# Window attention and convolution block: score rows four partitions apart, and half of the value copy on DVE

## Chip, core and metric

One NeuronCore of one Trainium2 chip runs the whole kernel in one launch. The metric is the device time of that launch in microseconds (us). Engines are named as in the profile: PE is the matrix engine (PEld its weight loads), DVE the vector engine, ACT the scalar engine, POOL the GpSimd engine, SP the queue that issues most transfers.

## What is computed

```
x: 32 x 96 x 56 x 56 float32; windows of 7 x 7 = 49 tokens; 12 heads of 8 channels
xn   = layernorm(x over channels) * g + b                  # per token
q,k,v= xn @ qkv_w.T + qkv_b
attn = softmax(q * 8**-0.5 @ k.T + bias_table[rel])        # 49 x 49 per head and window
x2   = x + (attn @ v) @ proj_w.T + proj_b
c    = batchnorm(depthwise_conv3x3(x2))
out  = c + gelu(c @ w1.T + b1) @ w2.T + b2                 # 96 -> 384 -> 96
```

## The kernel before

**Chunks and steps.** The image rows are cut into 256 chunks (CHUNKS), 8 per image; a chunk is 7 image rows, 96 channels by 392 pixels, which is 8 windows. The program is a software pipeline written out by hand, one function `step` per engine: in one step the layernorm works on chunk e, the q, k, v products on chunks e-1 and e-2, the row maxima on e-2, the exponentials and the product with v on e-3 and e-4, the projection on e-5, the convolution taps on e-6 and e-7, the two dense layers on e-7 and e-8. There are 264 steps. Eight are written out ahead, then a loop (`run`, line 168) goes 30 times over a body of eight steps and jumps back, then the rest is written out. Nothing schedules: each engine takes its instructions in the order written, and semaphores hold it.

**How the scores are made.** float32 products are split into float16 parts, high and low (`kh`, `kl`, `qh`, `ql`, each 96 rows by 512, row = d * 12 + head for the 8 elements d of a head). For one head, a score is a single matmul whose contraction rows are held in two buffers, `k_all` and `q_all`, four slots deep, [123, 4, 12 heads, 512]. The first 49 rows (and 49 rows from 64) hold the one-hot keys against the bias (high and low part); eight rows each from partition 48+, 56+ and 112+ hold the three terms high*high, low*high and high*low; two rows hold what the 48+ rows overwrite; row 122 holds the row maximum against -1. `max_scores` (line 318) uses rows 0 to 121 and gives the scores whose maxima DVE takes (`maxima`, line 671, L676); `exp_scores` (line 304) uses all rows and gives score minus maximum for ACT's exp (L501).

**The score transfers.** [...] SP issues six of them per step (`term`, line 239, issue at L242), 96 KB each, 8 destination partitions of 12 KB:

```
TERM = (48, 56, 112)
sp.dma_start(t[TERM[n]:TERM[n] + HD, c % 4, :, :], part[:, c % 2, :]).then_inc(exp_in[c % 4], 16)
```

SP's order in a step (line 244) is: the maxima row (L252), the load of x (L256), kh twice, qh twice, kl, then a wait for `y_done`, ql, and the store of y (L272). The first `max_scores` of a step waits for all six transfers of its chunk (`exp_in`). `y` (DVE, L729) is the last result of chunk e-8 and is waited for by SP before ql goes out.

**The value copy.** `values` (PE, line 387) makes v for two windows at a time, the one on PSUM partitions 0 to 48, the other on 64 to 112. ACT copies both to `v32` (L555, two ACTIVATEs), every fourth float of the destination. Then ACT squares the centred input (L560, waited for by PE's `variance`, L361), and PE's `projection` (L409) may overwrite the PSUM bank once the copy is done.

**Setup.** DVE clears `k_all`, sets rows of -1 (L624, L625), and after the loads copies the one-hot and bias rows into four slots, the two row groups apart (L661, L663, 16 copies); POOL clears `q_all`. Four small transfers then move the two spare rows (L224), and SP waits for them.

Of the kernel before, what the change touches and what calls it, by code (L numbers as in the profile page):

```python
# [7 lines left out]
F32, F16 = mybir.dt.float32, mybir.dt.float16  # L8
# [3 lines left out]
HD = C // HEADS  # L12
# [10 lines left out]
WP = 64  # L23
TERM = (48, 56, 112)
LAST = (120, 121)
MAXROW = 122
ROWS = 123
NG = HEADS // 4
# [5 lines left out]
UP = 256.0  # L34
LOADS = 22
UN = CPI


def block_program(nc, x, w_qkv, b_qkv_row, b_v, w_proj, w_proj_rows, b_proj, ln_g, ln_b, bias_q,
                  conv_w, bn_g, bn_b, bn_mean, bn_var, w1, b1, w2, b2, eye, out):  # L40
    ctx = ExitStack()
    with ctx:
# [6 lines left out]
        def sems(name, n):  # L49
# [9 lines left out]
        center, avg = sb("center", [C, C]), sb("avg", [C, C])  # L59
        hot_f, hot_h = sb("hot_f", [64 + TOK, WP]), sb("hot_h", [64 + TOK, WP], F16)  # L60
        g_c, b_c, bv_c, bng_c, bnb_c, bnm_c, bnv_c, b2_c = (cols[:, i:i + 1] for i in range(8))
# [22 lines left out]

        bias_f = p32[0:64 + TOK, 0, :, :]
        bias_h = o_sb[0:64 + TOK, 0, :, :].rearrange("p g t -> p (g t)").bitcast(F16)[:, 0:HEADS * TOK].rearrange("p (h t) -> p h t", t=TOK)
        bias_l = o_sb[64:64 + TOK, 1, :, :].rearrange("p g t -> p (g t)").bitcast(F16)[:, 0:HEADS * TOK].rearrange("p (h t) -> p h t", t=TOK)
        rows_f, wq_f = y[:, 0, 0:3 * C], y[:, 1, 0:3 * C]
# [19 lines left out]
        dve_setup, act_setup, pe_setup, pool_setup = sem("dve_setup"), sem("act_setup"), sem("pe_setup"), sem("pool_setup")  # L108
        ready, shift_done, rows_set = sem("ready"), sem("shift_done"), sem("rows_set")
        x_in = sems("x_in", 4)  # L110
# [89 lines left out]
        def _(sp):  # L200
# [79 lines left out]
        def _(pe):  # L280
# [117 lines left out]
            def projection(st):  # L398
# [85 lines left out]
        def _(act):  # L484
# [55 lines left out]
            def step(st):  # L540
# [72 lines left out]
        def _(dve):  # L613
# [39 lines left out]

            for rows in (slice(0, TOK), slice(64, 64 + TOK)):
                v.tensor_copy(hot_h[rows, :], hot_f[rows, :])
                link(v.tensor_copy(bias_h[rows, :, :], bias_f[rows, :, :]))
            link(v.tensor_tensor(bias_l, bias_f[64:64 + TOK, :, :], bias_h[64:64 + TOK, :, :], ALU.subtract))
            dve.wait_ge(pool_setup, 2)
            for r in range(4):
                for rows, part in ((slice(0, TOK), bias_h[0:TOK, :, :]), (slice(64, 64 + TOK), bias_l)):  # L660
                    v.tensor_copy(k_all[rows, r, :, :].rearrange("p h (w t) -> p (h w) t", t=WP),  # L661
                                  hot_h[rows, :].unsqueeze(1).broadcast_to([TOK, HEADS * NW, WP]))
                    v.tensor_copy(q_all[rows, r, :, :].rearrange("p h (w t) -> p h w t", t=WP)[:, :, :, 0:TOK],  # L663
                                  part.unsqueeze(2).broadcast_to([TOK, HEADS, NW, TOK]))
            for r in range(2):
# [46 lines left out]
            def step(st):  # L712
# [84 lines left out]
```

## Time and profile before

| | |
|---|---|
| three runs | 4474.67, 4489.48, 4498.07 us (median 4489.48) |
| profiled execution, own time | 4491.72 us |
| its span | 4489.9 us (1.8 us around it) |
| granted PE clock, mean | 0.941 |
| PE busy | 3754.7 us, 84% |
| ACT busy | 3323.4 us, 74% |
| DVE busy | 2753.7 us, 61% |
| POOL busy | 1201.4 us, 27% |
| queue of SP's transfers | 36.1% of 16 engines' span |

A busy share is an average over the span. `A <- B` after an idle time names what the profile takes to have ended it; "issue" means that it shows no such thing. The granted clock is 1.00 at 2.4 GHz and 0.50 at 1.2 GHz. L numbers are lines of the kernel before.

### The profile page before, as it was taken

The numbers are of one execution on the slowest core, as the hardware profiler recorded it, in microseconds if no ns is written. First come the engines' busy times: TensorE is split into PE (matmuls) and PEld (weight loads), VectorE is DVE, ScalarE is ACT, GpSimd is POOL, SyncE is SP. The second block draws the span as 40 slices with busy tenths as digits, with TensorE's granted clock in tenths as the row PEclk, the third lists the DMA queues.
The fourth block names the chain that finished last, engine by engine and source line by source line (L and its number), as shares of the span: only waits on it lengthen the run. The fifth ranks groups of instructions, "written<-read, shape, count | busy, mean of one in ns | idle before, by whom it ended". The sixth has DMA issues, their size and how long they took to land.

```text
span 4489.9 us, 198689 instructions
## 1 busy us (share of the span) xinstructions
PE 3754.7 (84%) x83724; PEld 2432.7 (54%) x83724; DVE 2753.7 (61%) x4908; ACT 3323.4 (74%) x5379; POOL 1201.4 (27%) x1550
## 2 busy tenths in 40 slices
PE   2788888888888888888888888888888888888887
PEld 1555555555555555555555555555555555555554
DVE  6466566666555666666565665666665665556666
ACT  1578777777777777777777777777777777778787
POOL 1222222222222222222222222222222222222222
PEclk9899899999889999999999988999999998899999
DMA  1444444444444444444444444444444444444442
GB/s 29 64 73 78 72 73 75 76 74 75 67 69 76 75 72 73 74 76 74 72 76 70 78 69 70 75 75 76 73 73 72 78 75 71 70 74 79 75 78 50
DMA packets 269485, 322.72 MB, mean 72 GB/s; under 512 B 54991, under 2 KB 252048, under 8 KB 268594
## 3 DMA queue, kind: packets, MB, share of 16 engines
q1 hardware_dynamic: 235826, 232.32, 36.1%
q0 software_dynamic: 32768, 77.14, 7.0%
q8 instruction: 729, 11.94, 1.3%
q14 instruction: 162, 1.33, 0.1%
HBM read 39.35 MB, written 38.54 MB: 17 GB/s over the span
## 4 chain that ended last, share of the span: by engine, by line
DMA 28%; PE 28%; issue 15%; ACT 12%; DVE 10%; SPq 6%; ACTq 0%; DVEq 0%; POOL 0%; POOLq 0%
DMA q_all<-ql 28%; SPq L242 6%; PE sm_ps L327 6%; PE a_ps L440 6%; DVE mx L676 4%; PE o_ps L343 3%; DVE s L698 3%; PE st_ps L312 2%; PE a_ps L361 2%; ACT g L538 2%; PE b_ps L285 2%; ACT sq L564 1%; ACT v L555 1%; ACT sq L566 1%; ACT sq L560 1%
## 5 line engine op out<-in xcount | busy, mean ns | idle before, releaser
L676 DVE TENSOR_REDUCE mx<-sm_ps 128x12 f16<-128x588 f32 x1024 | 782.7, 764 | 967.1 <-PE sm_ps L327 966.8
L698 DVE SCALAR_TENSOR_TENSOR s<-ximg,cols,s 96x392 f32<-96x392 f32 x2048 | 1262.0, 616 | 13.1 <-POOL s L600 2.9
L600 POOL TENSOR_TENSOR s<-ximg,cols 96x392 f32<-96x392 f32 x256 | 281.0, 1098 | 2897.9 <-DVE y L729 2897.9
L327 PEld LDWEIGHTS sm_ps<-k_all,q_all 122*64 122x64 f16 x24576 | 505.9, 118 | 605.0 <-DMA q_all<-ql 351.1
L327 PE MATMUL sm_ps<-k_all,q_all 122*64 122x49 f16 x24576 | 617.5, 197 | 254.6 <-DMA q_all<-ql 241.9
L501 ACT ACTIVATE p<-st_ps 128x588 f32<-128x588 f32 x1024 | 666.2, 651 | 208.1 <-PE st_ps L312 205.4
L440 PE MATMUL a_ps<-g,w_s 128*96 128x392 f32 x1536 | 677.7, 555 | 0.0
L607 POOL DMA_DIRECT2D ox<-o_sb x1024 | 580.7, 569 | 59.3 <-issue 39.2
L312 PE MATMUL st_ps<-q_all,k_all 123*64 123x49 f16 x24576 | 580.5, 193 | 6.3 <-issue 6.3
L312 PEld LDWEIGHTS st_ps<-q_all,k_all 123*64 123x64 f16 x24576 | 493.8, 115 | 158.8 <-issue 155.4
L343 PE MATMUL o_ps<-p,v 128*32 128x49 f32 x24576 | 439.1, 213 | 150.9 <-DVE mx L676 145.8
L735 DVE TENSOR_TENSOR xn<-d_ps,sq 96x392 f32<-96x392 f32 x256 | 143.9, 562 | 668.3 <-ACT sq L566 668.3
L343 PEld LDWEIGHTS o_ps<-p,v 128*32 128x32 f32 x24576 | 332.0, 112 | 372.5 <-DVE mx L676 181.1
L521 ACT ACTIVATE o_sb<-o_ps 128x294 f32<-128x294 f32 x512 | 213.0, 416 | 327.8 <-PE o_ps L343 327.3
L555 ACT ACTIVATE v<-b_ps 49x384 f32<-49x384 f32 x512 | 445.0, 869 | 8.8 <-PE b_ps L287 2.5
L595 POOL TENSOR_TENSOR xl<-xn,xh 96x392 f16<-96x392 f32 x256 | 332.5, 1299 | 316.0 <-ACT xh L570 315.8
L361 PE MATMUL a_ps<-sq,avg 96*96 96x392 f32 x512 | 232.7, 537 | 140.4 <-ACT sq L560 140.4
L440 PEld LDWEIGHTS a_ps<-g,w_s 128*96 128x96 f32 x1536 | 261.5, 184 | 139.2 <-issue 115.9
L544 ACT ACT_TABLE_LOAD x256 | 328.4, 1283 | 4.6
L538 ACT ACT_TABLE_LOAD x256 | 328.4, 1283 | 4.4
L432 PE MATMUL b_ps<-s,w_s 96*128 96x392 f32 x512 | 229.6, 532 | 99.0 <-issue 98.6
L570 ACT ACTIVATE xh<-xn 96x392 f16<-96x392 f32 x256 | 138.2, 540 | 160.9 <-DVE xn L735 160.9
(96 smaller groups left out, 5396.8 us busy)
## 6 DMA issues: line engine op xcount, KB each, us to landing
ox<-o_sb POOLq DMA_DIRECT2D x1024, 73.5 KB, 5.3
k_all<-kh SPq DMA_DIRECT2D x512, 96.0 KB
q_all<-qh SPq DMA_DIRECT2D x512, 96.0 KB
x_sb<-in_x SPq DMA_DIRECT2D x256, 147.0 KB, 3.5
out<-y SPq DMA_DIRECT2D x256, 147.0 KB, 7.5
k_all<-kl SPq DMA_DIRECT2D x256, 96.0 KB
q_all<-ql SPq DMA_DIRECT2D x256, 96.0 KB
q_all<-mxt SPq DMA_DIRECT2D x256, 12.0 KB, 4.1
```

The source lines that it names most:

```text
L312: last = mm(st_ps[64 * w:64 * w + 64, h // HH, c0:c0 + TOK], k_all[:, r, h, n:n + WP], q_all[:, r, h, n:n + TOK], start=True, stop=True)
L327: last = mm(sm_ps[64 * w:64 * w + 64, h // HH, c0:c0 + TOK], q_all[0:MAXROW, r, h, n:n + WP], k_all[0:MAXROW, r, h, n:n + TOK], start=True ...
L343: last = mm(o_ps[32 * c4:32 * c4 + 32, at:at + TOK], v32[:, r, h, q, :], p32[:, q, h, :], start=True, stop=True)
L440: last = mm(a_ps[0:C, 0:CT], w2_s[:, k, :], g[:, k, :], start=k == 0, stop=k == NB - 1)
L501: af(p32[:, q, :, :].rearrange("p (b h) n -> p b h n", b=2), st_ps[:, :, 0:HALF].rearrange("p b (h n) -> p b h n", n=TOK), ACT.Exp).then_i ...
L538: af(g[:, k, :], (a_ps, d_ps, b_ps)[k][:, 0:CT], ACT.Gelu, bias=b1_c[:, k:k + 1]).then_inc(g_done, 1)
L544: act.preload_act_table_set("natural_log_exp_and_others")
L555: af(v32[64 * w:64 * w + TOK, (st[1] - 2) % 2, :, :, :].rearrange("p h n (d x) -> p (h n d) x", x=4)[:, :, w], b_ps[64 * w:64 * w + TOK, 0 ...
L595: tt(xl[0:C, r, :, 0:TOK], xn[:, :, :], xh[0:C, r, :, 0:TOK], ALU.subtract).then_inc(xl_done, 1)
L607: nc.gpsimd.dma_start(ox[:, r4, x4, :], o_sb[x4::4, r4, :, :]).then_inc(o_in[r4], 16)
L676: v.tensor_reduce(mx[:, (st[1] - lag) % 2, :, p].rearrange("p (b h) -> p b h", b=2), sm_ps[:, :, 0:HALF].rearrange("p b (h n) -> p b h n", ...
L698: v.scalar_tensor_tensor(acc, image_rows(st, lag, k // 3, k % 3), cw_c[:, k:k + 1], acc, ALU.mult, ALU.add)\
```

## The change

The contraction rows are laid out anew. The three terms interleave over partitions 0 to 31: term n takes partitions n, n+4, ..., n+28 (n = 0, 1, 2). The bias rows take the rest, the high part on 64 to 112, the low part in five pieces (32 to 63, 113 to 126, and 3, 7, 11); row 127 holds the maximum. The contraction is 127 and 128 rows instead of 122 and 123. SP's order and the six sizes stay. The copy of v on partitions 64 to 112 goes from ACT to DVE, behind y and ahead of tap 8, with a semaphore of its own. In the setup, the bias and one-hot rows are laid down once over 128 partitions (8 copies instead of 16), `k_all` isn't cleared, the four row transfers and their wait are gone, there are 31 loads instead of 22, and SP waits for three small memsets before the first load.

```diff
-TERM = (48, 56, 112)
-LAST = (120, 121)
-MAXROW = 122
-ROWS = 123
+ROWS = 128
+MAXROW = ROWS - 1
+TERMS = 4 * HD
+HIGH = ((2 * TERMS, 0, TOK),)
+LOW = ((TERMS, 0, 32), (2 * TERMS + TOK, 32, 14), (3, 46, 1), (7, 47, 1), (11, 48, 1))
...
+            for row, key, n in HIGH + LOW:
+                loads.append((bias_f[row:row + n, :, :], bias_q[key:key + n]))
+                loads.append((hot_f[row:row + n, :], eye[key:key + n, 0:WP]))
+            sp.wait_ge(blank, 3)
...
-            for t in (k_all, q_all):
-                for at, row in zip(LAST, (TOK - 1, 64 + TOK - 1)):
-                    sp.dma_start(t[at:at + 1, :, :, :], t[row:row + 1, :, :, :]).then_inc(rows_set, 16)
-            sp.wait_ge(rows_set, 16 * 4)
...
-                sp.dma_start(t[TERM[n]:TERM[n] + HD, c % 4, :, :], part[:, c % 2, :]).then_inc(exp_in[c % 4], 16)
+                sp.dma_start(t[n:TERMS:4, c % 4, :, :], part[:, c % 2, :]).then_inc(exp_in[c % 4], 16)
...
-                    for w in range(2):
-                        af(v32[64 * w:64 * w + TOK, (st[1] - 2) % 2, :, :, :].rearrange("p h n (d x) -> p (h n d) x", x=4)[:, :, w],
-                           b_ps[64 * w:64 * w + TOK, 0:NP * C], ACT.Identity, scale=1 / UP).then_inc(v32_done, 1)
+                    af(v32[0:TOK, (st[1] - 2) % 2, :, :, :].rearrange("p h n (d x) -> p (h n d) x", x=4)[:, :, 0],
+                       b_ps[0:TOK, 0:NP * C], ACT.Identity, scale=1 / UP).then_inc(v32a_done, 1)
...
-            link(v.memset(words(k_all[:]), 0.0))
-            link(v.memset(k_all[96:ROWS, :, :, :].rearrange("p r h (w t) -> p (r h w) t", t=WP)[:, :, 0:TOK], -1.0))
+            v.memset(bias_f, 0.0).then_inc(blank, 1)
+            v.memset(hot_f[:, :], 0.0).then_inc(blank, 1)
+            dve.wait_ge(blank, 2)
+            v.memset(hot_f[96:ROWS, 0:TOK], -1.0).then_inc(blank, 1)
...
             for r in range(4):
-                for rows, part in ((slice(0, TOK), bias_h[0:TOK, :, :]), (slice(64, 64 + TOK), bias_l)):
...
+                v.tensor_copy(k_all[:, r, :, :].rearrange("p h (w t) -> p (h w) t", t=WP),
+                              hot_h[:, :].unsqueeze(1).broadcast_to([ROWS, HEADS * NW, WP]))
+                v.tensor_copy(q_all[:, r, :, :].rearrange("p h (w t) -> p h w t", t=WP)[:, :, :, 0:TOK],
+                              bias_p.unsqueeze(2).broadcast_to([ROWS, HEADS, NW, TOK]))
...
+                if real(st, 2):
+                    wait(dve, v_done, st, 2)
+                    wait(dve, pv_done, st, 4, NP)
+                    v.tensor_scalar(v32[64:64 + TOK, e % 2, :, :, :].rearrange("p h n (d x) -> p (h n d) x", x=4)[:, :, 1],
+                                    b_ps[64:64 + TOK, 0:NP * C], 1 / UP, None, ALU.mult).then_inc(v32b_done, 1)
```

PE waits for `v32a_done` and `v32b_done` where it waited for `v32_done`, in `projection`, `values_times_p` and `keys`.

Two engines have another list of instructions in the steady steps. DVE, at the end of a step, before (L729 is y, L698 a tap, L735 the normalised input, L676 the maxima):

```order
L676 TENSOR_REDUCE mx<-sm_ps 128x12
L141 REGISTER_ALU
L698 SCALAR_TENSOR_TENSOR s<-ximg,cols,s 96x392
L729 SCALAR_TENSOR_TENSOR y<-a_ps,cols,s 96x392
L141 REGISTER_ALU
L698 SCALAR_TENSOR_TENSOR s<-ximg,cols,s 96x392
L141 REGISTER_ALU
L735 TENSOR_TENSOR xn<-d_ps,sq 96x392
```

DVE at the same place in the changed program (y is L731 there, xn L742):

```order
L678 TENSOR_REDUCE mx<-sm_ps 128x12
L142 REGISTER_ALU
L700 SCALAR_TENSOR_TENSOR s<-ximg,cols,s 96x392
L731 SCALAR_TENSOR_TENSOR y<-a_ps,cols,s 96x392
L736 TENSOR_SCALAR v<-b_ps 49x384
L142 REGISTER_ALU
L700 SCALAR_TENSOR_TENSOR s<-ximg,cols,s 96x392
L142 REGISTER_ALU
L742 TENSOR_TENSOR xn<-d_ps,sq 96x392
```

One instruction has come in between y and the eighth tap, ahead of xn and the last maxima. ACT, from the key and query copies (L530) to the logarithm of the layernorm (L564), before:

```order
L530 ACTIVATE kh<-b_ps 96x8x49
L530 ACTIVATE qh<-d_ps 96x8x49
L521 ACTIVATE o_sb<-o_ps 128x3x98
L501 ACTIVATE p<-st_ps 128x588
L555 ACTIVATE v<-b_ps 49x384 x2
L560 ACTIVATE sq<-d_ps 96x392
L501 ACTIVATE p<-st_ps 128x588
L564 ACTIVATE sq<-a_ps,cols 96x392
```

ACT at the same place in the changed program:

```order
L533 ACTIVATE kh<-b_ps 96x8x49
L533 ACTIVATE qh<-d_ps 96x8x49
L524 ACTIVATE o_sb<-o_ps 128x3x98
L504 ACTIVATE p<-st_ps 128x588
L557 ACTIVATE v<-b_ps 49x384
L562 ACTIVATE sq<-d_ps 96x392
L504 ACTIVATE p<-st_ps 128x588
L566 ACTIVATE sq<-a_ps,cols 96x392
```

One of the two copies ahead of the square is gone. PE's and SP's lists keep their order in the steady steps.

## Rows read from the trace of the kernel before

**Rows 1.** The page, span and busy time of each engine
```profile
PE 3754.7 (84%) x83724; PEld 2432.7 (54%) x83724; DVE 2753.7 (61%) x4908; ACT 3323.4 (74%) x5379; POOL 1201.4 (27%) x1550
```

**Rows 2.** Windows, one step each: start:end length, PE, PEld, DVE, ACT, POOL busy, granted clock, DMA
```profile
1845.83:1860.83 15.00, 13.83 (x329) 9.01 (x327) 10.45 (x20) 13.07 (x23) 4.68 (x6) 1.00 0.42 73
1860.83:1876.66 15.83, 13.45 (x327) 9.01 (x327) 10.43 (x20) 12.79 (x21) 4.69 (x6) 1.00 0.47 84
...
2126.59:2146.48 19.89, 16.47 (x327) 10.45 (x327) 10.66 (x21) 12.92 (x21) 4.68 (x6) 0.83 0.46 70
```

**Rows 3.** Windows: sum over 30 rounds, its last round, then sum over 29 jump steps
```profile
4164.26:4289.82 125.56, 109.71 (x2617) 72.33 (x2616) 83.38 (x152) 103.49 (x169) 37.05 (x48) 1.00 0.48 79
sum 4087.63, PE 3495.48 PEld 2268.00 DVE 2524.87 ACT 3112.57 POOL 1110.55; mean PE 116.52 PEld 75.60 DVE 84.16 ACT 103.75 POOL 37.02
...
sum 641.19, PE 510.74 PEld 312.50 DVE 312.94 ACT 382.24 POOL 133.52; mean PE 17.61 PEld 10.78 DVE 10.79 ACT 13.18 POOL 4.60
```

**Rows 4.** Chain that ended last, one link; start us, us, what
```profile
2009.32 0.63 DVE y L729
...
2009.97 8.08 DMA q_all<-ql
```

**Rows 5.** Timeline of PE at that place; start us, us, engine, line, what, idle before
```profile
2016.26 0.82 PE L432 MATMUL b_ps<-s,w_s 96*128 96x392 f32 x2
2018.09 0.56 PE L327 MATMUL sm_ps<-k_all,q_all 122*64 122x49 f16 x24 [1.01 <-DMA q_all<-ql]
```

**Rows 6.** Waits: whole span, then 60 to 202 us; total us, times, longest us
```profile
PE sm_ps L327 <- DMA q_all<-ql: 241.9, 175, 7.2
...
PE sm_ps L327 <- DMA q_all<-ql: 26.9, 7, 7.2
```

**Rows 7.** DMA, GB/s in 40 slices: 82 to 88 us, then 68 to 80 us
```profile
GB/s 48 61 82 109 62 48 55 55 117 96 142 246 128 51 68 89 41 41 48 55 41 61 55 55 48 55 55 55 48 48 61 55 55 55 55 55 55 55 89 86
...
GB/s 0 0 61 41 31 51 21 72 82 82 20 31 31 82 41 10 0 0 0 0 0 0 0 0 0 0 0 0 0 0 0 125 251 272 335 21 44 119 147 82
```

**Rows 8.** Timeline of one step that waits for no transfer
```profile
1845.07 1.74 ACT L555 ACTIVATE v<-b_ps 49x384 f32<-49x384 f32 x2
1845.54 0.82 PE L353 MATMUL d_ps<-x_sb,center 96*96 96x392 f32 x2
1845.83 0.62 DVE L729 SCALAR_TENSOR_TENSOR y<-a_ps,cols,s 96x392 f32<-96x392 f32 x1 [0.48 <-PE a_ps L440]
1846.30 0.56 PE L312 MATMUL st_ps<-q_all,k_all 123*64 123x49 f16 x24
1846.83 0.49 ACT L560 ACTIVATE sq<-d_ps 96x392 f32<-96x392 f32 x1
1847.45 0.89 PE L361 MATMUL a_ps<-sq,avg 96*96 96x392 f32 x2 [0.59 <-ACT sq L560]
1849.56 0.56 DVE L735 TENSOR_TENSOR xn<-d_ps,sq 96x392 f32<-96x392 f32 x1 [2.58 <-ACT sq L566]
1850.86 0.47 PE L343 MATMUL o_ps<-p,v 128*32 128x49 f32 x24 [0.58 <-DVE mx L676]
```

**Rows 9.** Groups by form; count, busy us, mean ns, idle before
```profile
L707 DVE SCALAR_TENSOR_TENSOR kl<-b_ps,kh 96x392 f16<-96x392 f32 x256 | 143.6, 561 | 8.3 <-ACT kh L530 8.3
```

**Rows 10.** Timeline of the setup, ACT, DVE and PE
```profile
13.26 0.29 ACT L490 ACTIVATE cols<-cols 96x1 f32<-96x1 f32 x1 [11.21 <-DMA hot_f<-in_eye]
17.79 15.74 DVE L625 MEMSET k_all<- 27x18816 f16 x1 [3.98 <-issue]
...
39.34 1.75 DVE L661 COPY k_all<-hot_h 49x6144 f16<-49x6144 f16 x1
41.01 1.43 DVE L663 COPY q_all<-o_sb 49x4704 f16<-49x4704 f16 x1
...
64.67 0.38 DVE L667 MEMSET v<- 49x384 f32 x1 [0.39 <-issue]
...
67.47 1.62 PE L353 MATMUL d_ps<-x_sb,center 96*96 96x392 f32 x2 [31.30 <-DVEq L669]
```

More of the change, by code:

```diff
@@ L34 @@
 UP = 256.0
-LOADS = 22
+LOADS = 31
 UN = CPI
 def block_program(nc, x, w_qkv, b_qkv_row, b_v, w_proj, w_proj_rows, b_proj, ln_g, ln_b, bias_q,
-                  conv_w, bn_g, bn_b, bn_mean, bn_var, w1, b1, w2, b2, eye, out):
+                  conv_w, bn_g, bn_b, bn_mean, bn_var, w1, b1, w2, b2, eye, low, out):
     ctx = ExitStack()
@@ L59, in block_program @@
         center, avg = sb("center", [C, C]), sb("avg", [C, C])
-        hot_f, hot_h = sb("hot_f", [64 + TOK, WP]), sb("hot_h", [64 + TOK, WP], F16)
+        hot_f, hot_h = sb("hot_f", [ROWS, WP]), sb("hot_h", [ROWS, WP], F16)
+        low_c = sb("low_c", [ROWS, 1])
         g_c, b_c, bv_c, bng_c, bnb_c, bnm_c, bnv_c, b2_c = (cols[:, i:i + 1] for i in range(8))
@@ L83, in block_program @@
         y = sb("y", [97, 2, CT])
-        bias_f = p32[0:64 + TOK, 0, :, :]
-        bias_h = o_sb[0:64 + TOK, 0, :, :].rearrange("p g t -> p (g t)").bitcast(F16)[:, 0:HEADS * TOK].rearrange("p (h t) -> p h t", t=TOK)
-        bias_l = o_sb[64:64 + TOK, 1, :, :].rearrange("p g t -> p (g t)").bitcast(F16)[:, 0:HEADS * TOK].rearrange("p (h t) -> p h t", t=TOK)
+        bias_f = p32[:, 0, :, :]
+        bias_h, bias_p = (o_sb[:, i, :, :].rearrange("p g t -> p (g t)").bitcast(F16)[:, 0:HEADS * TOK].rearrange("p (h t) -> p h t", t=TOK) for i in range(2))
         rows_f, wq_f = y[:, 0, 0:3 * C], y[:, 1, 0:3 * C]
@@ L108, in block_program @@
         dve_setup, act_setup, pe_setup, pool_setup = sem("dve_setup"), sem("act_setup"), sem("pe_setup"), sem("pool_setup")
-        ready, shift_done, rows_set = sem("ready"), sem("shift_done"), sem("rows_set")
+        ready, shift_done, blank = sem("ready"), sem("shift_done"), sem("blank")
         x_in = sems("x_in", 4)
@@ L118, in block_program @@
             "q_done", "k_done", "qh_done", "kh_done", "ql_done", "kl_done"))
-        v_done, v32_done = sem("v_done"), sem("v32_done")
+        v_done, v32a_done, v32b_done = sem("v_done"), sem("v32a_done"), sem("v32b_done")
         sm_done, max_done, mxt_done, mxt_out = sem("sm_done"), sem("max_done"), sem("mxt_done"), sem("mxt_out")
@@ L205, in _ @@
                 (w2_s[:, :, :], w2), (eye_f[:, :], eye),
-                (bias_f[0:TOK, :, :], bias_q), (bias_f[64:64 + TOK, :, :], bias_q),
-                (hot_f[0:TOK, :], eye[0:TOK, 0:WP]), (hot_f[64:64 + TOK, :], eye[0:TOK, 0:WP]),
-            ]
+                (low_c[:, :], low),
+            ]
+            for row, key, n in HIGH + LOW:
+                loads.append((bias_f[row:row + n, :, :], bias_q[key:key + n]))
+                loads.append((hot_f[row:row + n, :], eye[key:key + n, 0:WP]))
+            sp.wait_ge(blank, 3)
             for dst, src in loads:
@@ L334, in values_times_p @@
                 if q == 0:
-                    wait(pe, v32_done, st, lag, 2)
+                    wait(pe, v32a_done, st, lag)
+                    wait(pe, v32b_done, st, lag)
                 wait(pe, p_done, st, lag, NP, q + 1)
@@ L378, in keys @@
                     wait(pe, kl_done, st, 2)
-                    wait(pe, v32_done, st, 3, 2)
+                    wait(pe, v32a_done, st, 3)
+                    wait(pe, v32b_done, st, 3)
                     wait(pe, sum_done, st, 6)
@@ L403, in projection @@
                 if real(st, 2):
-                    wait(pe, v32_done, st, 2, 2)
+                    wait(pe, v32a_done, st, 2)
+                    wait(pe, v32b_done, st, 2)
                 else:
@@ L652, in _ @@
             v.scalar_tensor_tensor(wq_l[:, :], wq, UP, wq_h[:, :], ALU.mult, ALU.subtract)
[L654 to L657, printed above, removed]
+            v.tensor_copy(hot_h[:, :], hot_f[:, :])
+            link(v.tensor_copy(bias_h, bias_f))
+            link(v.scalar_tensor_tensor(bias_p, bias_h, low_c[:, :], bias_f, ALU.mult, ALU.add))
             dve.wait_ge(pool_setup, 2)
             for r in range(4):
-                for rows, part in ((slice(0, TOK), bias_h[0:TOK, :, :]), (slice(64, 64 + TOK), bias_l)):
[L661 to L664, printed above, removed]
+                v.tensor_copy(k_all[:, r, :, :].rearrange("p h (w t) -> p (h w) t", t=WP),
+                              hot_h[:, :].unsqueeze(1).broadcast_to([ROWS, HEADS * NW, WP]))
+                v.tensor_copy(q_all[:, r, :, :].rearrange("p h (w t) -> p h w t", t=WP)[:, :, :, 0:TOK],
+                              bias_p.unsqueeze(2).broadcast_to([ROWS, HEADS, NW, TOK]))
             for r in range(2):
@@ L772 @@
     w_qkv, b_qkv, w_proj = a(L0_conv_qkv_w), a(L0_conv_qkv_b), a(L0_conv_proj_w).T
+    low = np.zeros((ROWS, 1), np.float32)
+    for row, key, n in LOW:
+        low[row:row + n] = -1.0
     col = lambda v: a(v).reshape(C, 1)
@@ L788 @@
         "eye": np.eye(128, dtype=np.float32),
+        "low": low,
     }
```

## The prediction

> **What bounds the kernel now.** The page's first part comes first: PE is busy 84% of the span, ACT 74%, DVE 61% [rows 1]. No engine is full, so the question is what ends the waits within a step. I cut the span at the starts of y (once per chunk) and asked for the busy time of each piece. The shortest ordinary steps take 15.00 us, the common ones 15.83 us; a third kind takes 19.89 us with the same instructions at a mean granted clock of 0.83, so part of it ran at 1.2 GHz [rows 2]. Thirty rounds of eight steps sum to 4087.6 us, 29 steps with the loop's jump among them to 641.2 us [rows 3]. That leaves 211 ordinary steps with 3446.4 us, 16.33 us each, and 22.11 us for a jump step.
>
> Then the chain of waits. At the common step it goes from y (start 2009.32) to the ql transfer, 8.08 us from 2009.97, and from it to the first score matmul of the next step [rows 4]. PE's timeline shows what this costs: its last matmul of the step ends at 2016.26 + 0.82 = 2017.08, the next starts at 2018.09, and 1.01 us of waiting is put down to the transfer [rows 5]. Over the span that wait sums to 241.9 us in 175 places, 26.9 us of it before 202 us, while the pipeline fills [rows 6]. In the 15.00 us step the transfer lands in time, and what is left is a wait of PE for ACT's square of 0.59 us, and one for the last maxima of 0.58 us [rows 8].
>
> Why the transfer takes 8 us when it moves 96 KB: the view of transfers shows a plateau. In the stretch where the first chunk's six score transfers drain, the rate lies at 48 to 61 GB/s in most slices, and above 100 only where the load of x runs with them; that load (96 partitions, alone) reaches 335 GB/s, and the very first score packets 147 GB/s [rows 7]. So the score transfers queue at some 57 GB/s: 98304 B / 57 GB/s = 1.7 us each, 10.3 us for six, in a step of 15 us. ql is the last of the queue.
>
> **The score transfers (L242).** Six transfers of the same size and packets, onto rows four apart. What they can reach: from below in time, the 147 GB/s of the first packets, 0.67 us each; from above, today's 1.7 us, or worse, since no row shows such a pattern. I take 0.7 us, because the first packets go out fast and only then slow down, which is what a full path at the receiving end does, and the sending side is unchanged. Six then need 4.2 us instead of 10.3, so ql, issued last, lands some 3 to 4 us after y instead of 8 to 9. PE asks for it 2017.08 - 2009.32 = 7.8 us after y starts. So the wait goes with 4 us to spare, and even 1.3 us per transfer would do.
>
> The Trainium skill, "SBUF — State Buffer", Door 1: The DMA port swizzle, says that bits 4 to 2 and bit 6 of the partition pick one of 16 ports of about 27 GB/s. By it eight neighbours have two ports, an estimated 54 GB/s, and eight rows four apart have eight, an estimated 218 GB/s or 0.45 us per transfer. The plateau of 48 to 61 agrees with two ports [rows 7]; no row shows the eight.
>
> What is late next is the step as it looks without that wait: 15.00 us.
>
> **The value copy (L555, now half on DVE).** ACT's two copies take 1.74 us from 1845.07 to 1846.81, and the square starts at 1846.83, although PE's centred product, which it needs, ends at 1845.54 + 0.82 = 1846.36 [rows 8]. With one copy ACT is free at 1845.94, the square starts at 1846.37 and ends at 1846.86. PE's score matmuls ahead of the variance end at 1846.30 + 0.56 = 1846.86, so the variance starts at 1846.88 instead of 1847.45: **0.57 us** less per step. All that follows it (logarithm, exponential, xn, last maxima, the next step's start) hangs on it and moves along: 15.00 - 0.57 = **14.43 us**. PE's wait of 0.58 us for the maxima stays, since both ends move.
>
> On DVE the copy costs between 0.38 us, the memset of the same 49 x 384 destination [rows 10], and 0.56 us, a 392-element operation with a PSUM source and two inputs [rows 9]; I take 0.5, nearer to the one that reads PSUM. It stands between y and xn, where DVE idles 2.58 us [rows 8]. With xn due 0.57 us sooner 2.01 us of cover are left; 0.5 of it is used, nothing is added. If the cover were gone, 0.5 us x 256 = 128 us would come back. v itself is ready long before y, which needs later matmuls, so the added waits hold nobody; PE's projection, which waits for the copy, is behind the variance.
>
> **Contraction of 128 rows.** Priced at nothing: matmul time goes by columns here, 24 score matmuls in 0.56 us [rows 8]. The bound: if it went by rows, 4% of eight such groups, 0.18 us a step, 46 us in all.
>
> **Setup.** DVE now clears k_all and sets -1 until 17.79 + 15.74 = 33.5 us, reaches the copies at 39.34, needs four times two of 1.75 + 1.43 us, and PE starts at 67.47; the loads were there at 13.26 [rows 10]. In the change the loads end the wait: 9 more at 13.26 / 22 = 0.6 us each, and 3 us for the three small memsets ahead of them, make 21.7 us. Add 5.8 us of constants as now (33.5 to 39.3), 4 x 3.18 = 12.7 us of copies and the 2.8 us behind them: 43 us. That is 24 us earlier; between 15 (loads slower) and 30.
>
> **The sum**, against the profiled execution's own 4491.7 us:
> - 211 ordinary steps from 3446.4 to 211 x 14.43 = 3044.7: -401.7. The low clock costs 19.89 - 15.83 = 4.06 us in a step [rows 2]. It comes where PE idles; with that wait gone I expect nearly none of it, but keep five such steps, +20: **-382**.
> - 29 jump steps, which keep their hole and low clock, 0.57 each: **-16**.
> - after the loop's last round, about eight full steps like those of its last round, 125.56 / 8 = 15.70 [rows 3], to 14.43: **-10**.
> - setup: **-24**.
> - filling: most of the 26.9 us of waiting [rows 6]: **-20**.
>
> 4491.7 - 452 = **4039 us**. The median of the three runs shown is 4489.5, 2 us lower than the profiled run; against it this is -10%.
>
> **Rivals.**
> *The transfers are no faster* (0.05): what holds them at 57 GB/s is not where they land but how many engines carry them. For it: the load of x has more engines at work and goes faster. Against: the first packets of the same pattern reach 147 GB/s [rows 7]. Then ql still ends the step, the ACT saving hides behind it, and only setup and jump steps gain: 4491.7 - 40 = 4451. The Trainium skill, "DMA: Bandwidth & Descriptors", Why a DMA increments its semaphore by 16 and not by 1, has this rule: the number of engines is the largest up to 16 that divides the slowest dimensions of both sides. Here that is 8 of 96 and 8, before and after.
> *The 0.57 us do not come* (0.08): steps stop at 15.00 us because something else is due at the variance. For it: ACT is busy 13.07 us of that step and PE 13.83 [rows 2], there is little slack. Against: the timeline above. 248 steps x 0.57 = 141 us more: 4180.
> *Slower* (0.04): strided writes from eight engines collide with x, y and the ox transfers on the same places and each score transfer takes longer than today. Place: ql's landing, on the chain of 211 steps. It decides from 40 / (6 x 211) = 0.03 us more per transfer; at 0.1 us more: 4451 + 127 = 4578. For it: the six now share 32 partitions where they had three groups. Against: the groups don't overlap in time today, as the plateau shows.
> *The change does nothing* is no case: the lists of instructions show both parts.
>
> **How the numbers follow.** The forecast has 0.83, the rivals 0.05, 0.08 and 0.04. The first rival's 4451 is -0.9%, so a little of it counts as no change (0.5% is about what a measurement of this kernel can tell). Faster 0.94, same 0.02, slower 0.04. Around 4039: down 20 if no low clock is left, 6 for the setup, up to 50 if the jump's hole shrinks with emptier queues; up 46 for rows, 60 for 15 more low-clock steps, 141 for the second rival. The range is 3960 to 4185, which leaves out the first and third rival and the tails.
>
> **What would show it.** The wait of sm_ps for ql nearly gone; slices above 100 GB/s in the filling; ordinary steps at 14.4 us with a clock of 1.00; square and variance back to back; DVE's wait before xn near 1.5 us; PE's first step near 43 us. I am wrong if ordinary steps stay at 15.0 us, if DVE no longer idles before xn, or if ql still ends PE's wait.

## Result and profile after

| | before | after |
|---|---|---|
| median | 4493.14 us (4 runs, 4474.67 to 4498.07) | 3944.55 us (4 runs, 3941.15 to 3950.22) |
| ratio | | 0.8787 (95%: 0.8759 to 0.8815) |
| span of the profiled execution | 4489.9 us | 3942.9 us |
| granted PE clock, mean | 0.941 | 0.968 |

The forecast was 4039 us in a range of 3960 to 4185. The kernel gained more than the range allowed: 12.1% instead of 10%. First the page's busy times and the queue of SP's transfers after the change:

```profile
PE 3638.6 (92%) x83724; PEld 2351.4 (60%) x83724; DVE 2947.5 (75%) x5155; ACT 3111.2 (79%) x5123; POOL 1136.0 (29%) x1550
q1 hardware_dynamic: 235894, 232.12, 20.5%
```

Nearly the same bytes in nearly as many packets (235826 and 235894) take 20.5% of 16 engines' span instead of 36.1%. Worked out per packet: 0.361 x 16 x 4489.9 / 235826 = 0.110 us before, 0.205 x 16 x 3942.9 / 235894 = 0.055 us after.

The transfers of the first chunk, GB/s in 40 slices from 49 to 57 us (beside [rows 7]), then the waits for ql over the span and from 40 to 141 us (beside [rows 6]):

```profile
GB/s 0 0 0 0 0 0 0 82 118 148 123 77 82 128 159 87 118 148 143 143 138 164 154 118 164 128 108 118 188 238 297 216 84 31 0 0 0 0 0 0
```

```profile
PE sm_ps L327 <- DMA q_all<-ql: 4.9, 4, 2.0
```

No plateau near 57 is left. The six transfers run at 77 to 164 GB/s, and all is done within six microseconds of the first packet; the slices above 164 are those in which the load of x runs too. SP issues the six 0.7 us apart (0.72 us for 96 KB is 137 GB/s), so its issuing may well be what paces them now; no run tests that. Both answers for the waits read alike: all 4.9 us of waiting for ql lie in the filling. Before there were 241.9.

One round of the loop, cut at y as in [rows 2] (start:end, length, PE, PEld, DVE, ACT, POOL busy, granted clock, DMA share, GB/s), then the sum over thirty rounds and the sum over the 29 jump steps, as in [rows 3]:

```profile
1832.87:1847.44 14.57, 13.83 (x329) 9.01 (x327) 11.39 (x21) 12.18 (x21) 4.38 (x6) 1.00 0.22 66
1847.44:1861.79 14.35, 13.61 (x328) 8.93 (x327) 11.39 (x22) 12.11 (x20) 4.38 (x6) 1.00 0.30 87
1861.79:1876.06 14.27, 13.68 (x328) 8.93 (x327) 11.39 (x22) 12.10 (x20) 4.37 (x6) 1.00 0.29 86
...
1933.16:1953.08 19.92, 16.71 (x327) 10.35 (x327) 11.70 (x22) 12.33 (x20) 4.37 (x6) 0.83 0.26 75
```

```profile
sum 3617.70, PE 3388.55 PEld 2194.64 DVE 2741.95 ACT 2914.36 POOL 1047.52; mean PE 112.95 PEld 73.15 DVE 91.40 ACT 97.15 POOL 34.92
...
sum 595.05, PE 500.56 PEld 308.20 DVE 339.50 ACT 357.35 POOL 126.49; mean PE 17.26 PEld 10.63 DVE 11.71 ACT 12.32 POOL 4.36
```

The 211 ordinary steps take 3617.70 - 595.05 = 3022.65 us, 14.33 each, nearly all alike at 14.27; every one runs at 2.4 GHz. Within the thirty rounds low clock is left in the jump steps alone.

Around the variance (timeline; compare [rows 8]):

```profile
1618.29 0.86 ACT L557 ACTIVATE v<-b_ps 49x384 f32<-49x384 f32 x1
1618.79 0.82 PE L354 MATMUL d_ps<-x_sb,center 96*96 96x392 f32 x2
1619.31 0.62 DVE L731 SCALAR_TENSOR_TENSOR y<-a_ps,cols,s 96x392 f32<-96x392 f32 x1
1619.65 0.50 ACT L562 ACTIVATE sq<-d_ps 96x392 f32<-96x392 f32 x1 [0.50 <-PE d_ps L354]
1619.95 0.85 DVE L736 TENSOR_SCALAR v<-b_ps 49x384 f32<-49x384 f32 x1
1620.20 0.90 PE L362 MATMUL a_ps<-sq,avg 96*96 96x392 f32 x2
1622.32 0.56 DVE L742 TENSOR_TENSOR xn<-d_ps,sq 96x392 f32<-96x392 f32 x1 [0.85 <-ACT sq L568]
1623.61 0.47 PE L344 MATMUL o_ps<-p,v 128*32 128x49 f32 x24 [0.51 <-DVE mx L678]
1633.07 0.82 PE L354 MATMUL d_ps<-x_sb,center 96*96 96x392 f32 x2
```

ACT now waits 0.50 us for PE before the square, where PE waited for ACT. From the centred product to the variance it is 1.41 us; before, 1847.45 - 1845.54 = 1.91. DVE's copy takes 0.85 us. PE's wait for the maxima is what is left in its step.

The setup (timeline): the loads are there at 15.86 us, where they end ACT's first wait, and DVE's eight copies begin at 23.71. PE then waits for DVE until 38.92, where it starts its first chunk, not at 67.47 [rows 10]. The forecast had the loads end at 21.7.

```profile
15.86 0.29 ACT L493 ACTIVATE cols<-cols 96x1 f32<-96x1 f32 x1 [13.82 <-DMA hot_f<-in_eye]
23.71 1.76 DVE L663 COPY k_all<-hot_h 128x6144 f16<-128x6144 f16 x1
38.92 1.62 PE L354 MATMUL d_ps<-x_sb,center 96*96 96x392 f32 x2 [18.97 <-DVEq L671]
```

### The profile page after: what moved, and what is told of

Its sections match the earlier page's. It is cut to its first block, busy times and chain, and to the rows that moved or that the text cites. A ratio compares the mean times of both kernels' runs of the same rounds, so it can differ in the third digit from the quotient of the medians.

```text
span 3942.9 us, 199136 instructions
## 1 busy us (share of the span) xinstructions
PE 3638.6 (92%) x83724; PEld 2351.4 (60%) x83724; DVE 2947.5 (75%) x5155; ACT 3111.2 (79%) x5123; POOL 1136.0 (29%) x1550
## 3 DMA queue, kind: packets, MB, share of 16 engines
q1 hardware_dynamic: 235894, 232.12, 20.5%
## 4 chain that ended last, share of the span: by engine, by line
PE 75%; ACT 11%; DVE 7%; issue 6%; SPq 1%; DMA 0%; POOL 0%; DVEq 0%; POOLq 0%; ACTq 0%
PE a_ps L443 14%; PE sm_ps L327 10%; PE o_ps L344 7%; PE a_ps L362 6%; PE a_ps L435 5%; PE st_ps L312 5%; DVE mx L678 5%; PE b_ps L435 5%; PE d_ps L354 4%; PE d_ps L435 4%; PE b_ps L285 4%; ACT sq L566 4%; ACT sq L568 3%; ACT sq L562 3%; PE b_ps L287 2%
## 5 line engine op out<-in xcount | busy, mean ns | idle before, releaser
L602 POOL TENSOR_TENSOR s<-ximg,cols 96x392 f32<-96x392 f32 x256 | 215.9, 844 | 2563.9 <-DVE y L731 2563.9
L327 PEld LDWEIGHTS sm_ps<-k_all,q_all 127*64 127x64 f16 x24576 | 486.1, 115 | 332.7 <-issue 236.4
L443 PE MATMUL a_ps<-g,w_s 128*96 128x392 f32 x1536 | 635.8, 525 | 0.0
L327 PE MATMUL sm_ps<-k_all,q_all 127*64 127x49 f16 x24576 | 595.0, 194 | 6.1 <-DMA q_all<-ql 4.9
L312 PEld LDWEIGHTS st_ps<-q_all,k_all 128*64 128x64 f16 x24576 | 483.3, 114 | 152.5 <-issue 148.5
L312 PE MATMUL st_ps<-q_all,k_all 128*64 128x49 f16 x24576 | 569.4, 192 | 0.5 <-issue 0.5
L344 PE MATMUL o_ps<-p,v 128*32 128x49 f32 x24576 | 432.4, 212 | 134.2 <-DVE mx L678 132.7
L742 DVE TENSOR_TENSOR xn<-d_ps,sq 96x392 f32<-96x392 f32 x256 | 143.9, 562 | 246.9 <-ACT sq L568 245.9
L443 PEld LDWEIGHTS a_ps<-g,w_s 128*96 128x96 f32 x1536 | 244.7, 173 | 120.9 <-issue 102.2
L435 PE MATMUL b_ps<-s,w_s 96*128 96x392 f32 x512 | 228.7, 530 | 78.0 <-issue 77.7
L562 ACT ACTIVATE sq<-d_ps 96x392 f32<-96x392 f32 x256 | 126.4, 494 | 151.7 <-PE d_ps L354 151.7
```

Of the source, the lines that this page charges most:

```text
L312: last = mm(st_ps[64 * w:64 * w + 64, h // HH, c0:c0 + TOK], k_all[:, r, h, n:n + WP], q_all[:, r, h, n:n + TOK], start=True, stop=True)
L327: last = mm(sm_ps[64 * w:64 * w + 64, h // HH, c0:c0 + TOK], q_all[0:MAXROW, r, h, n:n + WP], k_all[0:MAXROW, r, h, n:n + TOK], start=True ...
L435: mm(t[:, 0:CT], w1_s[:, k * 128:(k + 1) * 128], s2[0:C, (st[1] - lag) % 2, :], start=True, stop=True)\
L443: last = mm(a_ps[0:C, 0:CT], w2_s[:, k, :], g[:, k, :], start=k == 0, stop=k == NB - 1)
```

## Experiments

Most kernels here are the changed one with the edit shown. Three are the kernel before with an edit, and the last two build on an experiment ahead of them; the text says so each time. Ratios are to the kernel before, run on the same chip; where times of two experiments are compared, they can come from different chips, on which the kernel before had medians of 4493 to 4496 us.

### Where the rows lie

**Neighbouring rows.** The setup, the 128 rows and DVE's copy stay.

```diff
-LOW = (... , (3, 46, 1), (7, 47, 1), (11, 48, 1))
+LOW = (... , (24, 46, 1), (25, 47, 1), (26, 48, 1))
-sp.dma_start(t[n:TERMS:4, c % 4, :, :], part[:, c % 2, :])
+sp.dma_start(t[n * HD:n * HD + HD, c % 4, :, :], part[:, c % 2, :])
```

> The changed kernel with one thing undone: each transfer's eight rows are neighbours again (partitions 0-7, 8-15, 16-23; three low bias rows move to 24-26). Setup and the copy on DVE stay as changed. Theory, the landing places set the rate (the Trainium skill's port map: two ports of 16 for eight neighbours): packets of 1024 B back at about 130 ns, plateau near 57 GB/s, the wait for ql back, low clock back in ordinary steps, 4400 to 4450 us. Rival, the whole gain comes from the setup's layout, 128 rows and DVE's copy: stays within 1% of 3945 us.

Measured: 4479.12 us, ratio 0.998 (0.9947 to 1.0012): no difference from the kernel before that can be told from noise. Its lines (SP's transfers; then the wait for ql; then two steps, one at each clock):

```profile
q1 hardware_dynamic: 235894, 232.12, 35.8%
```

```profile
PE sm_ps L327 <- DMA q_all<-ql: 261.6, 178, 7.5
```

```profile
2077.09:2091.66 14.57, 13.83 (x329) 9.01 (x327) 11.37 (x21) 12.21 (x21) 4.37 (x6) 1.00 0.46 77
2091.66:2110.75 19.09, 16.53 (x328) 10.46 (x327) 11.58 (x21) 12.18 (x20) 4.36 (x6) 0.82 0.45 75
```

With the index of one transfer statement undone (three bias rows make room for it) the whole gain is gone: 4479 against 3945 us. That does not make the other parts worthless. The faster setup is still in this kernel, and so is DVE's copy; low clock in more steps takes back what they bring. Packets are back at 0.358 x 16 x 4467.2 / 235894 = 0.108 us. The median was outside the stated 4400 to 4450 by 0.7%: more steps fell to low clock than I had reckoned with, which the next part takes up.

**Two apart, sixteen apart.**

```diff
-t[n:TERMS:4, c % 4, :, :]
+t[(0, 1, 16)[n]:(0, 1, 16)[n] + 15:2, c % 4, :, :]     # two apart; low bias rows at 17, 19, 21
+t[n:n + 113:16, c % 4, :, :]                           # sixteen apart; bias in nine pieces, 37 loads
```

> The changed kernel with rows two apart (partitions 0,2,..14; 1,3,..15; 16,18,..30). Port map: four ports, an estimated 109 GB/s, 0.9 us per transfer; packets near 80 to 90 ns on average. Six then take 5.4 us, in time for the next step: 3945 us within 0.5%. If the time goes with the distance in some other way, packets lie anywhere between 56 and 134 ns.

> The changed kernel with rows sixteen apart (n, n+16, .. n+112), bias rows in 13-row pieces between them, 37 loads in the setup. Port map: again four ports, although the rows span the whole memory: packets as with two apart, 80 to 90 ns, not 56; time 3945 us plus some 3 us for six more loads. Rival, distance alone helps: packets at 56 ns or below, as with four apart.

Measured: 3952.16 us (0.8799, 0.8768 to 0.8830) and 3954.25 us (0.8807, 0.8775 to 0.8839). SP's transfers in the two, first two apart, then sixteen:

```profile
q1 hardware_dynamic: 235894, 232.12, 23.3%
```

```profile
q1 hardware_dynamic: 236010, 232.12, 26.5%
```

Per packet that is 0.062 and 0.071 us, against 0.055 with four apart and 0.108 as neighbours. These means take in x, y and the rows of maxima. The trace also has every packet by itself, and those of 1024 bytes on this queue are the score packets alone (96 packets x 6 transfers x 256 chunks = 147456):

| rows | mean score packet, ns | times as fast as neighbours |
|---|---|---|
| before (48+, 56+, 112+) | 134.5 | |
| neighbours | 131.9 | 1.0 |
| sixteen apart | 77.4 | 1.7 |
| two apart | 65.1 | 2.0 |
| four apart | 55.7 | 2.4 |

Rows sixteen apart span the whole memory and are served worse than rows four apart within 32 partitions, so distance is not the rule. The Trainium skill, "SBUF — State Buffer", Door 1: The DMA port swizzle, gives a formula for the port of a partition; worked out by it, neighbours reach two ports, two and sixteen apart four, four apart eight. The runs agree in order. They do not agree in size: twice the ports made packets 1.7 to 2.0 times as fast, four times the ports 2.4 times, and the 80 to 90 ns expected for four ports were 65 and 77. The median packet is 46 ns both with two and with four apart, so there something other than the number of ports sets the rate; what it is, no run shows. Two apart is a little better than sixteen, which the same map allows: there the third term has four other ports than the first two, with sixteen all three share the same four. That reason is not tested by itself.

The time hardly differs, because all three land ql in time: PE needs it 7.8 us after y. The packet time at which it comes too late lies between 77 and 132 ns.

### What the value copy brings

**Both copies on ACT again, rows four apart.**

```diff
                     af(v32[0:TOK, ...], b_ps[0:TOK, 0:NP * C], ACT.Identity, scale=1 / UP).then_inc(v32a_done, 1)
+                    af(v32[64:64 + TOK, ...], b_ps[64:64 + TOK, 0:NP * C], ACT.Identity, scale=1 / UP).then_inc(v32b_done, 1)
-                    v.tensor_scalar(v32[64:64 + TOK, ...], b_ps[64:64 + TOK, 0:NP * C], 1 / UP, None, ALU.mult).then_inc(v32b_done, 1)
```

> The changed kernel with both value copies on ACT again; rows stay four apart. Theory: PE's step goes from 14.28 to 14.78 us, as ACT's square ends 0.5 us later: 248 steps x 0.50 = +124 us, 4069 us. Rival, the copy is hidden once the transfers are fast: 3945 us.

Measured: 4037.71 us, ratio 0.8990 (0.8958 to 0.9023), so with fast transfers the copy is worth 93 us where 124 were expected. One of its steps:

```profile
1902.56:1917.25 14.69, 13.60 (x328) 9.02 (x327) 10.42 (x20) 12.86 (x22) 4.61 (x6) 1.00 0.28 84
```

The step is 14.70 us, not 14.78. The copy brings 14.70 - 14.27 = 0.43 us a step.

**Old rows, DVE's copy alone** (the kernel before, with the v32 lines of the change and nothing else).

> The kernel before with one thing changed: DVE copies the values on partitions 64 to 112, behind y; rows and setup stay old. Theory: the transfers end most steps, so the copy's 0.5 us a step hide; ordinary steps without low clock from 15.64 to about 15.1 (as with neighbouring rows in the new layout), low clock in more of them; 4450 to 4510 us, no gain over 0.5%. Rival, the two parts add: 4493 - 101 = 4392 us.

Measured: 4594.88 us, ratio 1.0216 (1.0173 to 1.0259): **slower**, by 1.7 to 2.6%. Neither theory had this. Its round of the loop:

```profile
2161.07:2175.93 14.86, 13.58 (x328) 9.01 (x327) 11.35 (x20) 12.04 (x21) 4.37 (x6) 1.00 0.50 79
2175.93:2195.17 19.24, 15.52 (x328) 9.77 (x327) 11.62 (x22) 12.47 (x21) 4.37 (x6) 0.91 0.46 70
2195.17:2209.94 14.77, 13.58 (x328) 9.01 (x327) 11.35 (x21) 12.03 (x21) 4.36 (x6) 1.00 0.49 77
2209.94:2229.22 19.28, 16.43 (x328) 10.56 (x327) 11.61 (x22) 12.25 (x21) 4.37 (x6) 0.82 0.46 70
...
2260.57:2279.60 19.03, 16.71 (x328) 10.48 (x327) 11.60 (x21) 12.24 (x21) 4.36 (x6) 0.82 0.48 71
```

```profile
PE sm_ps L327 <- DMA q_all<-ql: 285.9, 171, 6.7
```

Steps at full clock are shorter than before (14.8 us in this round; over the trace 15.0 on average instead of 15.6), and three of the round's seven ordinary ones fall partly to 1.2 GHz and cost 19. Counted over the ordinary steps of the trace by the clock's records, 86 of 211 have low clock against 37 in the kernel before (64 with neighbouring rows in the new layout). ACT no longer holds PE up by 0.5 us before the variance; PE's wait for ql grows from 241.9 to 285.9 us in all. The count of such steps is sensitive: the kernel with neighbouring rows also has slow transfers and DVE's copy and runs 116 us faster than this one (125 in the profiled executions: 25 by the first y, mostly the setup, and 92 in the ordinary steps, 64 of which have low clock instead of 86). Which of the layout's differences (the places of the rows, 128 of them instead of 123) does that is not shown.

**Useless work in that wait.** Two kernels: the one just told, and the kernel before, each with

```diff
                 t = (a_ps, d_ps, b_ps)[k]
+                if k == 2:
+                    mm(t[:, 0:CT], w1_s[:, k * 128:(k + 1) * 128], s2[0:C, (st[1] - lag) % 2, :], start=True, stop=True)
                 mm(t[:, 0:CT], w1_s[:, k * 128:(k + 1) * 128], s2[0:C, (st[1] - lag) % 2, :], start=True, stop=True)\
```

> The kernel of e5_old (old rows, half of the value copy on DVE) and PE makes the third hidden product twice (the same result, 0.66 us), just ahead of its wait for ql. Theory: low clock comes from that wait; with useless work in its place it goes from 86 ordinary steps to under 20, each worth 4 to 5 us, while the steps at full clock grow from 15.0 to at most 15.6: 4592 - 66 x 4.5 + 211 x 0.4 = 4380 us, faster for more work. Rival, low clock has another cause: 86 steps keep it and the time rises to 4600 to 4730 us.

> The kernel before with the same useless product. Theory: its 37 ordinary steps with low clock become under 10, 27 x 4.06 = 110 us less, at up to 0.3 us more in the others: 4493 - 110 + 60 = 4440 us. Rival: above 4500 us.

Measured: 4472.76 us (0.9949, 0.9932 to 0.9967) and 4502.53 us (1.0015, 0.9993 to 1.0037). Of the first, a part of its round of the loop, and its wait for ql:

```profile
2131.36:2147.11 15.75, 14.26 (x330) 9.38 (x329) 11.36 (x21) 12.28 (x21) 4.38 (x6) 1.00 0.51 78
2147.11:2162.88 15.77, 14.33 (x330) 9.39 (x329) 11.35 (x21) 12.38 (x21) 4.38 (x6) 1.00 0.51 79
...
2210.22:2233.56 23.34, 18.56 (x330) 11.33 (x329) 11.70 (x21) 12.49 (x21) 4.37 (x6) 0.78 0.34 57
```

```profile
PE sm_ps L327 <- DMA q_all<-ql: 197.7, 177, 6.6
```

With the old rows and DVE's copy, a useless product of 0.66 us per step makes the kernel **about 120 us faster** (ratio 1.0216 to 0.9949). Steps with low clock go from 86 to 29. So most of the low clock came from PE's idling ahead of that matmul. The 4380 expected was too low, since the steps at full clock grew from 15.0 to 15.7 on average, more than reckoned, and fewer steps lost the low clock.

Is it the length of a wait in one piece that counts, or a step's idle time as a whole? No run separates them. In the traces, the longest idle of PE in an ordinary step has a median of 2.3 us where the step has low clock and 0.6 us where it has none (in the kernel before 2.2 and 1.0), but in the filled kernel the two come close, 1.2 and 0.8.

On the kernel before the trade comes out even: low clock falls from 37 steps to 18 and PE's wait for ql from 241.9 to 133.7 us, as the theory has it, but the steps at full clock grow from 15.6 to 15.9. The 4440 was wrong, and the time is the rival's (above 4500, within noise of no change), though not for want of the effect.

**A denser destination.** Both copies write 384 floats in a row into a buffer of their own; v32 holds ones.

```diff
-v32[64:64 + TOK, e % 2, :, :, :].rearrange("p h n (d x) -> p (h n d) x", x=4)[:, :, 1]
+v_x[64:64 + TOK, :]
```

> The changed kernel, but both value copies write 384 floats in a row into a buffer of their own that nobody reads, and v32 holds only ones, so the output isn't the attention's. Theory: the destination's step of four floats makes the copies cost 0.86 us; dense they take 0.45 to 0.55 us on both engines. Rival, what costs is reading these PSUM partitions: 0.86 us stays. The time of the kernel stays at 3945 within 0.5%, since ACT waits 0.5 us before its square and DVE 0.85 before xn.

Measured: 3945.56 us, ratio 0.8770 (0.8751 to 0.8789), as the changed kernel. By form, after the change, then here (count, busy us, mean ns):

```profile
L557 ACT ACTIVATE v<-b_ps 49x384 f32<-49x384 f32 x256 | 220.1, 860 | 1.9 <-PE b_ps L287 1.9
L736 DVE TENSOR_SCALAR v<-b_ps 49x384 f32<-49x384 f32 x256 | 219.9, 859 | 8.7 <-PE b_ps L287 0.8
```

```profile
L737 DVE TENSOR_SCALAR v_x<-b_ps 49x384 f32<-49x384 f32 x256 | 143.4, 560 | 9.6 <-PE b_ps L288 1.7
L558 ACT ACTIVATE v_x<-b_ps 49x384 f32<-49x384 f32 x256 | 123.3, 482 | 2.4 <-PE b_ps L288 2.3
```

The destination's step of 16 bytes costs 0.30 us on DVE and 0.38 us on ACT. It is the step and not the other buffer: in the next experiment DVE writes that buffer with a step of four and takes 862 ns. In the changed kernel both copies' extra time is hidden. The Trainium skill, "SBUF — State Buffer", Specifications, speaks of lines of 16 bytes and a penalty for each crossing to a new one, which fits these two. The memset of the same destination takes 0.38 us [rows 10], less than either dense copy, so no such price shows there, and that line isn't the whole of it.

**The copy made twice.**

```diff
+v.tensor_scalar(v_x[64:64 + TOK, :].rearrange("p (a x) -> p a x", x=4)[:, :, 1], b_ps[64:64 + TOK, 0:NP * C], 1 / UP, None, ALU.mult)
 v.tensor_scalar(v32[64:64 + TOK, ...], b_ps[64:64 + TOK, 0:NP * C], 1 / UP, None, ALU.mult).then_inc(v32b_done, 1)
```

> The changed kernel, and DVE makes one more copy of the same 49 x 384 values (into a buffer that nobody reads, same step of four) ahead of the copy proper. If DVE's idle 0.85 us before xn is the cover, the second 0.86 us is just absorbed: 3945 to 3965 us, with that idle time gone. If the copy already costs time on the path, it doubles: +0.3 us a step or more, above 4010 us.

Measured: 3995.03 us, ratio 0.8885 (0.8859 to 0.8911); 50 us for 220 us of extra work, between the two expectations. The waits say why:

```profile
PE b_ps L413 <- DVE v L739: 128.0, 251, 2.2
...
DVE xn L745 <- ACT sq L569: 70.1, 224, 5.2
```

DVE's wait before xn falls from 245.9 to 70.1 us as the cover is used, but PE's projection, which overwrites the copied bank, now waits for the copy in 251 of 256 steps. With one copy it waits 2.7 us in all. At the same time PE's wait for the last maxima falls from 132.7 to 2.8 us; how the two make up the 50 us isn't worked out. So the projection is the first limit on the copy, not xn: the forecast had dismissed it with "behind the variance".

### A version that beats both

**Maxima first.** After the change PE waits 0.51 us a step for the last maxima, which stand behind xn on DVE.

```diff
+                maxima(st, 2, 3)
                 if real(st, 0):
                     wait(dve, rstd_done, st, 0)
...
-                maxima(st, 2, 3)
...
+                exp(st, 3, 2)
                 if real(st, 0):
                     wait(act, xn_done, st, 0)
...
-                exp(st, 3, 2)
```

> The changed kernel with the last maxima ahead of xn on DVE, and the third exponential ahead of xh on ACT. Theory: PE's wait of 0.51 us for the maxima is what is left in its step; it goes, and the step falls from 14.28 to 13.8 us where ACT follows (its slack is 0.43): 3945 - 248 x 0.45 = 3833 us. Rival, ACT and the chain through xn, xh, xl take its place: 3945 us or above.

Measured: 3902.90 us, ratio 0.8675 (0.8656 to 0.8694). The wait for the maxima is gone, but only 42 us come. In its timeline y and what waits for it:

```profile
1621.41 0.56 DVE L688 TENSOR_TENSOR ox<-ox,inv 96x392 f32<-96x392 f32 x1 [0.59 <-ACT inv L515]
1624.59 0.62 DVE L731 SCALAR_TENSOR_TENSOR y<-a_ps,cols,s 96x392 f32<-96x392 f32 x1
1625.35 0.87 PE L362 MATMUL a_ps<-sq,avg 96*96 96x392 f32 x2 [0.19 <-DVE y L731]
```

DVE had become late: it idles 0.59 us for ACT's inverse, runs without a break to y, and the variance, which reuses y's bank, waits for y.

**And the sixth tap into that gap.**

```diff
+                tap(st, 7, 6)
                 normalise(st)
                 low_part(st, b_ps, kh, kl, kh_done, kl_done)
-                tap(st, 7, 6)
```

> The reordered kernel of e9_both, and DVE takes the sixth tap ahead of the normalising product, where it idled 0.59 us for ACT's inverse. Theory: y was then the last thing the variance waited for; it comes 0.5 us sooner, PE's step falls by its wait of 0.17 us and what the chain through y held back, to 13.9 to 14.05 us: 3903 - 248 x 0.2 = 3853 us (3840 to 3880). Rival, ACT's own chain (o_sb, two table loads, three gelus, exp, inverse) holds the step at 14.19: 3903 us.

Measured: 3865.16 us, ratio 0.8598 (0.8583 to 0.8612): 2.0% below the changed kernel and 14% below the kernel before. A step (windows):

```profile
1833.14:1847.03 13.89, 13.68 (x328) 9.01 (x327) 11.68 (x22) 12.03 (x21) 3.95 (x6) 1.00 0.32 90
```

PE is busy 13.68 of 13.89 us, so it is the bound now.

> The kernel of e10_order with ACT's xh behind the copy of o_ps. Theory: o_sb and the table load no longer wait 0.2 us for xn, up to 0.2 us a step less than e10_order if ACT's chain holds the step, 3800 to 3850 us; rival, the same time as e10_order.

That kernel has ACT's xh behind `outputs(st, 3, 0)`. Measured: 3883.80 us, ratio 0.8640 (0.8616 to 0.8663), slower than the one before it by 19 us. The theory falls. In its trace ACT's copy of o_ps now waits for PE 157.4 us in all (67.9 in the kernel before it), the gelus come about 0.1 us later, and PE's weight load for the next query product waits for them in 207 places, 47.8 us in all, where it didn't wait before. Ordinary steps take 13.99 us on average instead of 13.90.

## Right and wrong, step by step

Forecast and measured, in the parts of the sum (profiled executions, us):

| part | forecast | measured |
|---|---|---|
| 211 ordinary steps | -382 | 3446.4 to 3022.7: -424 |
| 29 jump steps | -16 | 641.2 to 595.0: -46 |
| after the loop's last round | -10 | 200.1 to 183.8: -16 |
| setup | -24 | 67.47 to 38.92: -29 |
| filling, to the first y | -20 | 134.7 to 102.5: -32 |
| sum | -452 | -547 |

**The mechanism held; the sizes did not, and the time fell 15 us below the range.** The landing places set the rate of the score transfers, the wait for ql went, the square followed the centred product at once, and low clock left the ordinary steps. The 0.7 us per transfer instead of 1.7 was about right: score packets took 55.7 ns instead of 134.5, the same factor of 2.4. The rival of the engines' number falls with neighbouring rows at 4479 us, since that kernel's transfers have the same eight rows of 12 KB and differ in the partitions alone; the one of 15.00 us and the slower one didn't come. Of the 95 us that were missed, 42 lie in the ordinary steps, 30 in the jump steps, 12 in the filling, 6 and 5 in the rest.

**The step that failed is "what is late next is the step as it looks without that wait: 15.00 us".** I cut at y, and the y that opens that step had waited 0.48 us for PE [rows 8], while the next y (1860.83) had not; the piece was not one period of the engine that bounds. PE's centred product starts at 1845.54 there [rows 8] and next at

```profile
1860.32 0.82 PE L353 MATMUL d_ps<-x_sb,center 96*96 96x392 f32 x2
```

which makes 14.78 us. Both copies on ACT with fast transfers ran 14.70. The 0.57 us for the copy was 0.50 in the timeline and 0.43 in the experiment, so that term was too large, and the two errors partly cancelled. Together: 14.27 instead of 14.43, and no low clock at all, where I had kept 20 us. Over 211 steps the base brings 63 us more and the low clock 20; the copy takes 30 back, and 12 go because the steps' mean is 14.33.

**The jump steps** are the second term that was too small: they gained 1.59 us each instead of 0.57. Part is the same base (0.7); another is the hole at the jump: PE's waits put down to issue ahead of the third hidden product fall from 98.6 to 77.7 us,

```profile
PE b_ps L435 <- issue: 77.7, 29, 3.6
```

0.72 us per jump. I had it as a tail of the range ("if the jump's hole shrinks with emptier queues") and not in the sum. One run bears on it: with neighbouring rows and nothing else changed, these waits come to 103.7 us and the jump steps to 622.6 / 29 = 21.5 us against 20.5. So the transfers' landing changes the hole, by 0.9 us per jump. By what way is not shown, and it is not the only thing that does: the hole is 69.4 us with both copies on ACT and 88.0 in the fastest kernel, at fast transfers in both.

**The filling** gained more than its waits for ql (26.9 us), because there, too, the value copy and other waits of each chunk went. **The copy on DVE** cost 0.86 us, outside my bounds of 0.38 and 0.56: neither row had both a PSUM source and a destination step of four floats, and ACT's own row with 0.87 was the nearest. It cost no time, as the cover was large enough: DVE still idles 0.85 us before xn, where I had named 1.5.

**The rows' count** was rightly priced at nothing: PE's score groups still take 0.56 us for 24. **The setup** came 5 us better because nine more loads and three memsets cost 2.6 us (13.26 to 15.86), not 8.4; the constants took longer.

**A cause that the forecast did not have** is that work taken off ACT can bring more low clock. It said "it comes where PE idles", but priced rival one (transfers no faster) at 4451 us, a gain of 40. Neighbouring rows are that case: 4479 us, no gain that can be told. The copy by itself, with either rows (the lower row of the table has the new setup too):

| | both copies on ACT | half on DVE |
|---|---|---|
| old rows | 4493 | 4595 |
| rows four apart | 4038 | 3945 |

The same edit costs 102 us in one row and brings 93 in the other. In rival one the copy should have had a price, not a hidden saving.

## What to carry to other kernels

Here the places that a small transfer reached set its rate, by a factor of 2.4; before anything is rewritten around a late transfer, try other partitions for its rows. It need only be in time: two apart did as well as four. A wait removed ahead of a longer one doesn't shorten the step by itself: the time joins the longer wait, and here that cost PE its clock in more steps, so take the longest wait away first. To read a period off a trace, cut at the engine that bounds, at an instruction which did not wait.

## What the runs showed of the hardware that I had not expected

- Moving a copy of 0.86 us per step from ACT to DVE, with slow transfers as before, made the kernel slower (1.0216, 1.0173 to 1.0259), with 86 instead of 37 of 211 ordinary steps partly at 1.2 GHz; 0.66 us of useless matmul per step then made it about 120 us faster.
- A copy of 384 floats per partition from PSUM takes 0.86 us on either engine where the destination steps 16 bytes, and 0.56 (DVE) or 0.48 us (ACT) where it is dense.
- Of equal transfers into eight rows, sixteen apart over the whole memory is slower (77 ns per score packet) than four apart within 32 partitions (56 ns); neighbours take 132 ns.
